# All tiles written out without a loop, the state product on the state itself in two array halves, and new orders on every engine

## Chip, cores and metric

One core of one Trainium2 chip runs the whole program. The metric is the device time of one execution in microseconds. TensorE (PE in the rows, with PEld for its weight loads), VectorE (DVE), ScalarE (ACT), GpSimd (POOL) and SyncE (SP), which issues all transfers, each work through a list of instructions of their own, in order. They wait for each other by semaphores.

## What is computed

An mLSTM layer with eight heads, in the role of cross attention, and then a gated feed-forward layer whose operands are rounded to blocks of FP4. Batch 8, sequence 1024, width 512, hidden width 1408.

```python
x = x + mlstm(layernorm(x), ctx, ctx, igate_w, igate_b, fgate_w, fgate_b, norm_w)
x = x + ffn(layernorm(x), w_gate, w_up, w_down)
# mlstm, per head of 64 columns: q from x, k = v = ctx
log_D = tril(log_f_cum[:, None] - log_f_cum[None, :] + ig[None, :])
C = (q @ k.T / 8) * exp(log_D - max_log_D)
h = C / (max(abs(C.sum(-1)), exp(-max_log_D)) + 1e-6) @ v     # then a norm per head
# ffn: quant() rounds blocks of 16 to the FP4 grid, times max/6 of the block
gate, y = quant(x) @ quant(w_gate).T, quant(x) @ quant(w_up).T
out = quant(silu(gate) * y) @ quant(w_down).T
```

## The kernel before

**Tiles.** The 8 x 1024 tokens are 64 tiles of 128 tokens. Tile t is the chunk t // 8 of the sequence of batch t % 8 (its slot). The attention is computed chunk by chunk: the pairs inside a chunk as a 128 x 128 matrix per head, and everything older by a state of 64 x 65 numbers per head (`St`, one per slot; the 65th column sums the weights). Heads come in four pairs (`HC` = 4); a pair's two heads lie on partitions 0 to 63 and 64 to 127.

**A tile's way.** Load x and ctx, layer norm, transposes (`pe_x_T`, `pe_c_T`), gates (`pe_gate_mm`, and for every four tiles together `pe_pick_mm`, scans on VectorE, `pe_row_T`), then the scores (`pe_qk`), the decay matrix `D` (ScalarE exponential, GpSimd mask, VectorE product with the scores), the output product `pe_u`, the state's update (`pe_st_mm`, `dve_Sd` decays the state, `dve_St` adds), the norm per head (uc, sq, vr, ve, sch, hn), the residual `x1`, the second layer norm, quantising to `xqs` (a high and a low f16 part, ending in `dve_x_lo`), a transpose by transfer to `xqT` (`sp_xqT`), the gate and up products (`pe_gu`, in three pieces of 512, 512 and 384 columns; its first matmul of each group of six is L482), silu and product (h), quantising again (h_t, h_q, h_qs, h_hi, h_lo), a transpose by transfer (`sp_hqT`, three pieces), the down product (`pe_down`, L597 to L599) and the store.

**Turns.** The work is pipelined by hand. In turn u each engine works on several tiles of different age: TensorE on the gate and up product of tile u-8, the transposes and gates of u-1, the output product and state of u-6, the down product of u-9, the scores of u-5. The order inside a turn is written out in `pe_turn`, `act_turn`, `pool_turn`, `dve_turn` and `sp_turn`. TensorE's is gu piece 0, c_T, x_T, row_T, gu 1, gates, gu 2, u, down 0, st_mm, down 1, qk, down 2. Ahead of turn 10 stand start lists written out by hand (`pe_start` and so on), in which the three weights are quantised and the first tiles begin. Turns 10 to 18 and 59 to 74 are straight code. Turns 19 to 58 are a loop of five rounds with eight turns each (`turns`); in it a `Tile` carries the loop's register j, and each semaphore value, and each address of a transfer, is register arithmetic (`Tile._plus`, `tokens`). In the loop and outside it the order is the same.

**The output product.** `pe_u` adds, into two PSUM banks (`U`), the product of the decayed queries `xw` with the state and that of `D` with the values. For the first it uses `Sbd`, a copy of the state in which a pair's two heads stand on the diagonal of a 128 x 130 block with zeros beside them, so that one matmul over all 128 rows serves two heads. `act_Sbd` makes that copy, in two instructions for each tile; `dve_Sd` may change the state once it is made. The scores (`pe_qk`, L500) have no such copy: they contract over 64 rows, even heads on the upper and odd heads on the lower half of the array, into two banks. `pe_st_mm` (L583) writes 64 columns of the array a head.

Of the kernel before, what the change touches and what calls it, by code (L numbers as in the profile page):

```python
# [27 lines left out]
class Tile:  # L28


    def __init__(self, first, j=None):
        self.first, self.j = first, j
# [4 lines left out]
    def live(self, total):  # L37
        return self.j is not None or 0 <= self.first < total

    def at_start(self, n):  # L40
        return self.j is None and self.first == n

    def has(self, back):
        return self.j is not None or self.first >= back

    def back(self, d):
        return Tile(self.first - d, self.j)

    def _plus(self, value, per_loop):
        return value if self.j is None else self.j * per_loop + value  # L50

    def done(self, back=0, k=1):

        return self._plus(k * (self.first - back + 1), 8 * k)

    def of(self, k, i):

        return self._plus(k * self.first + i + 1, 8 * k)

    def dma(self, ring, back=0):  # L60

        return self._plus(16 * ((self.first - back) // ring + 1), 16 * (8 // ring))

    def quads(self, back=0):

        return self._plus((self.first - back) // 4 + 1, 2)

    def quads_of(self, k, i, back=0):

        return self._plus(k * ((self.first - back) // 4) + i + 1, 2 * k)  # L70

    def quad(self):
        return self._plus(self.first // 4, 2)

    def chunk(self):
        return self._plus(self.first // 8, 1)


def mlstm_fp4_ffn(nc, x, ctx_in, ig_w, ig_b, fg_w, fg_b, norm_w, w_gate, w_up, w_down, out):
# [22 lines left out]
    def tokens(t):  # L102
        return bass.ds(t.chunk() * P + t.slot * S, P)

    with ExitStack() as stack:
# [48 lines left out]
        Sbd = sb("Sbd", [P, HC, 2, DA])  # L154
# [73 lines left out]
        def pair(t, n):  # L228
# [14 lines left out]
            "go", "fill", "const", "g_in", "g_sum", "gT_ps", "gT", "pick", "zero",  # L243
# [9 lines left out]
            "D", "xw", "vc", "vk", "qk", "u", "st_mm", "Sd", "St", "sq", "un",  # L253
# [13 lines left out]
        s_mask, s_C, s_uc, s_Sbd = ([sem(f"s_{k}{n}") for n in range(2)] for k in ("mask", "C", "uc", "Sbd"))  # L267
# [7 lines left out]
        LOOP0, LOOPS = 19, 5  # L275
        LAST = NT + 11
# [13 lines left out]

        def sp_wait(e, s, value):
# [1407 lines left out]
```

## Time and profile before

| | us |
|---|---|
| median of three runs | 1970.78 (1965.21 to 1971.99) |
| the profiled execution | 1977.65 |
| its span, first to last instruction | 1975.9 |
| mean granted TensorE clock | 0.971 of 2.4 GHz |

An engine's busy time counts its own instructions, without waits, branches and the issuing of transfers. A matmul's record begins when it begins to stream and goes on until its modelled end, so neighbours overlap; the distance between starts is what a matmul takes. An f32 product makes two weight loads and two matmul records, an f16 product one of each. An idle time is put down to what was last to arrive.

### The profile page before, as it was taken

What the parts mean: (1) busy time and instruction counts of PE and PEld (TensorE: products, weight loads), DVE (VectorE), ACT (ScalarE), POOL (GpSimd) and SP (SyncE); (2) the same over time, 40 slices, a digit from 0 to 9 for tenths busy, and PEclk for the clock granted to TensorE, in tenths of its full rate; (3) what the DMA queues carried; (4) which work ended last, traced back from release to release, by engine and by line L of the source; (5) the groups of instructions that cost most, each with busy time, mean ns of one, the idle gap of its engine ahead of it and who ended that gap; (6) DMA issues with size and microseconds to landing.
All of it is one profiled execution on the core that took longest, in us unless ns stands there. A gap on an engine that the chain in (4) does not pass through costs nothing. (4 is left out here: it accounts for less than half of the span.)

```text
span 1975.9 us, 41157 instructions
## 1 busy us (share of the span) xinstructions
PE 1829.6 (93%) x12001; PEld 1031.1 (52%) x12001; DVE 1455.9 (74%) x3213; ACT 1452.2 (73%) x2990; POOL 1167.6 (59%) x1189
## 2 busy tenths in 40 slices
PE   2448999999999999999999999999999999999997
PEld 1334555555555555554555555555555555555553
DVE  8788777777777677776777777777777777778784
ACT  5767687787877777786777777777777877776663
POOL 7675655656565656655565655656566555655652
PEclk9758999999999999999999999999999999999999
DMA  6844444444344434444354443444344444444423
GB/s 198 177 107 103 99 117 110 115 111 115 102 116 110 118 102 116 100 114 106 101 120 106 116 102 101 116 110 118 98 111 109 107 115 113 109 102 94 103 64 71
DMA packets 366406, 218.40 MB, mean 111 GB/s; under 512 B 299168, under 2 KB 305824, under 8 KB 366144
## 3 DMA queue, kind: packets, MB, share of 16 engines
q1 hardware_dynamic: 366144, 215.40, 43.9%
q8 instruction: 105, 1.72, 0.4%
q14 instruction: 157, 1.29, 0.2%
HBM read 126.45 MB, written 17.30 MB: 73 GB/s over the span
## 5 line engine op out<-in xcount | busy, mean ns | idle before, releaser
L1041 POOL TENSOR_TENSOR stage<-stage,hs 128x512 f32<-128x512 f32 (+1 forms) x192 | 224.3, 1168 | 437.5 <-DVE stage L1249 433.3
L482 PE MATMUL bank<-wgTh,xqT 128*128 128x512 f16 (+1 forms) x768 | 281.2, 366 | 27.1 <-DMA xqT<-xqs 23.3
L483 PE MATMUL bank<-wuTh,xqT 128*128 128x512 f16 (+1 forms) x768 | 280.0, 365 | 0.0
L484 PE MATMUL bank<-wgTl,xqT 128*128 128x512 f16 (+1 forms) x768 | 279.7, 364 | 0.0
L487 PE MATMUL bank<-wuTh,xqT 128*128 128x512 f16 (+1 forms) x768 | 279.7, 364 | 0.0
L485 PE MATMUL bank<-wuTl,xqT 128*128 128x512 f16 (+1 forms) x768 | 279.5, 364 | 0.0
L486 PE MATMUL bank<-wgTh,xqT 128*128 128x512 f16 (+1 forms) x768 | 279.3, 364 | 0.0
L597 PE MATMUL bank<-wdTh,work 128*128 128x512 f16 x704 | 268.8, 382 | 11.0 <-DMA work<-stage 11.0
L598 PE MATMUL bank<-wdTl,work 128*128 128x512 f16 x704 | 267.6, 380 | 0.0
L599 PE MATMUL bank<-wdTh,work 128*128 128x512 f16 x704 | 267.5, 380 | 0.0
L1303 DVE TENSOR_TENSOR stage<-stage 128x512 f16<-128x512 f32 (+1 forms) x192 | 156.9, 817 | 102.5 <-ACT stage L723 102.4
L855 ACT ACTIVATE work<-stage 128x512 bf16<-128x512 f32 (+1 forms) x192 | 114.0, 594 | 152.4 <-POOL stage L1094 139.8
L1268 DVE SCALAR_TENSOR_TENSOR stage<-bank,wfix,stage 128x512 f32<-128x512 f32 (+1 forms) x192 | 133.3, 694 | 121.9 <-ACT stage L733 120.8
L1260 DVE TENSOR_TENSOR D<-bank,D 128x512 f32<-128x512 f32 x128 | 88.2, 689 | 160.3 <-POOL D L1034 133.2
L1094 POOL TENSOR_TENSOR stage<-stage,hinv 128x512 f32<-128x512 f32 (+1 forms) x192 | 190.0, 991 | 10.7 <-DVE hinv L1334 10.7
L1029 POOL TENSOR_TENSOR sch<-ve,mhalf 128x8 f32<-128x8 f32 x64 | 106.2, 1659 | 105.6 <-DVE ve L1457 105.6
L733 ACT ACT_TABLE_LOAD x126 | 161.7, 1283 | 3.2 <-PE bank L487 1.1
L680 ACT ACTIVATE D<-mb,cols 128x128 f32<-128x128 f32 x512 | 156.3, 387 | 4.1 <-DMA mb<-max_dram 2.9
L1077 POOL TENSOR_TENSOR xn<-xn,xs 128x512 f32<-128x512 f32 x64 | 68.2, 1065 | 141.0 <-DVE xn L1315 141.0
L571 PE MATMUL bank<-vc,D 128*128 128x65 f32 x1024 | 147.1, 268 | 0.0
L733 ACT ACTIVATE stage<-bank,wfix 128x512 f32<-128x512 f32 (+1 forms) x192 | 124.7, 649 | 24.4 <-PE bank L487 22.6
L571 PEld LDWEIGHTS bank<-vc,D 128*128 128x128 f32 x1024 | 140.1, 198 | 0.0
(191 smaller groups left out, 4252.2 us busy)
## 6 DMA issues: line engine op xcount, KB each, us to landing
mb<-max_dram SPq DMA_DIRECT2D x64, 512.0 KB, 3.9
xb<-in_x_dram SPq DMA_DIRECT2D x64, 256.0 KB, 2.8
cf<-in_ctx_dram SPq DMA_DIRECT2D x64, 256.0 KB, 2.7
cn<-in_ctx_dram SPq DMA_DIRECT2D x64, 256.0 KB, 3.0
x<-in_x_dram SPq DMA_DIRECT2D x64, 256.0 KB, 3.1
wb<-warp_dram SPq DMA_DIRECT2D x128, 128.0 KB, 2.9
out_dram<-ob SPq DMA_DIRECT2D x64, 256.0 KB, 3.1
work<-stage SPq DMA_TRANSPOSE x192, 3.1
```

Of the source, the lines that this page charges most:

```text
L482: e.matmul(g[:, 0:w], hi, wgT[0][:, c, n0:n0 + w], start=first, stop=False)
L483: e.matmul(y[:, 0:w], hi, wuT[0][:, c, n0:n0 + w], start=first, stop=False)
L484: e.matmul(g[:, 0:w], hi, wgT[1][:, c, n0:n0 + w], start=False, stop=False)
L485: e.matmul(y[:, 0:w], hi, wuT[1][:, c, n0:n0 + w], start=False, stop=False)
L486: e.matmul(g[:, 0:w], lo, wgT[0][:, c, n0:n0 + w], start=False, stop=last)
L487: i = e.matmul(y[:, 0:w], lo, wuT[0][:, c, n0:n0 + w], start=False, stop=last)
L571: i = e.matmul(o[:, par, :], D[:, par, c, :], vc[t.parity][:, 2 * c + par, :], start=False, stop=(c % 2 == 1 and par == 1))
L597: e.matmul(DOWN[:, :], hi, wdT[0][:, c0 + c, :], start=(c0 + c == 0), stop=False)
L598: e.matmul(DOWN[:, :], hi, wdT[1][:, c0 + c, :], start=False, stop=False)
L599: i = e.matmul(DOWN[:, :], lo, wdT[0][:, c0 + c, :], start=False, stop=(c0 + c == IC - 1))
L733: e.activation(sl[:, n0:n0 + w], pair(t, n)[0][:, 0:w], ACT.Silu, scale=wfix[:, 0:1]).then_inc(s_silu[n], 1)
L1041: e.tensor_tensor(blocks(hx[:, n0:n0 + w]), blocks(hx[:, n0:n0 + w]), per_block(hs2[:, n0 // BLOCK:(n0 + w) // BLOCK]), ALU.mult).then_inc ...
```

## The change

It does four things.

1. `turns` is one straight list of turns, 10 to 75. `Tile` has no register, all semaphore values and addresses are constants, and the helper `sp_wait` with its extra semaphore increment is gone, as is GpSimd's in `pool_mask`.
2. `Sbd`, `act_Sbd` and the filling of `Sbd` are gone. `pe_u` multiplies `xw` with `St` directly, a head at a time, over 64 rows: four heads first, on alternating halves and into alternating banks, then D's eight products, then the other four heads. TensorE waits for its own first group ahead of the last. `dve_Sd` now waits for u.
3. The orders inside a turn are new on every engine. TensorE's differs by x_T, row_T, c_T in place of c_T, x_T, row_T. SyncE takes x_in, cn_in (one turn later than before), rows_out (one turn later), the store (one turn later), hqT 0, hqT 1, x1_in, mb_in, hqT 2, xqT, c_in, wb_in. VectorE has hn at the end of its turn and not early in the next; GpSimd and ScalarE are below.
4. The start lists are new. They hold the same work but for a few steps at the seam to the first turn.

```diff
         def tokens(t):
-            return bass.ds(t.chunk() * P + t.slot * S, P)
+            return slice(t.first // 8 * P + t.slot * S, t.first // 8 * P + t.slot * S + P)
...
         def turns(e, turn):
-            for u in range(FIRST, LOOP0):
-                turn(e, u, None)
-            with e.Fori(0, LOOPS) as j:
-                for i in range(8):
-                    turn(e, LOOP0 + i, j)
-            for u in range(LOOP0 + 8 * LOOPS, LAST):
-                turn(e, u, None)
+            for u in range(FIRST, LAST):
+                turn(e, u)
...
-            e.wait_ge(s_Sbd[0], t.done())
-            e.wait_ge(s_Sbd[1], t.done())
+            if t.at_start(0):
+                e.wait_ge(S_["zero"], 1)
+            if t.has(8):
+                e.wait_ge(S_["St"], t.done(8))
             e.wait_ge(S_["xw"], t.done())
             e.wait_ge(S_["vc"], t.done())
             e.wait_ge(s_C[0], t.done())
             e.wait_ge(s_C[1], t.done())
+
+
+            def inter(c, par, **flags):
+                r = slice(par * DH, (par + 1) * DH)
+                return e.matmul(U[c // 2][:, c % 2, par, :], xw[r, c, :], St[t.slot][r, c, :], **flags)
+
+            for c in range(2):
+                even, odd = inter(c, 0, start=(c == 0), stop=False), inter(c + 2, 1, start=(c == 0), stop=False)
+            even.then_inc(S_["u_first"], 1)
+            odd.then_inc(S_["u_first"], 1)
             for c in range(HC):
-                o = U[c // 2][:, c % 2]
-                e.matmul(o.rearrange("p r d -> p (r d)"), xw[:, c, :], Sbd[:, c, :, :].rearrange("p r d -> p (r d)"),
-                         start=(c % 2 == 0), stop=False)
                 for par in range(2):
-                    i = e.matmul(o[:, par, :], D[:, par, c, :], vc[t.parity][:, 2 * c + par, :], start=False, stop=(c % 2 == 1 and par == 1))
+                    e.matmul(U[c // 2][:, c % 2, par, :], D[:, par, c, :], vc[t.parity][:, 2 * c + par, :], start=False, stop=False)
+            e.wait_ge(S_["u_first"], t.of(2, 1))
+            for c in range(2):
+                inter(c + 2, 0, start=False, stop=(c == 1))
+                i = inter(c, 1, start=False, stop=(c == 1))
             i.then_inc(S_["u"], 1)
...
-        def act_Sbd(e, t, par):
-            if t.at_start(0):
-                e.wait_ge(S_["zero"], 1)
-            if t.has(8):
-                e.wait_ge(S_["St"], t.done(8))
-            if t.has(1):
-                e.wait_ge(S_["u"], t.done(1))
-            r = slice(par * DH, (par + 1) * DH)
-            e.copy(Sbd[r, :, par, :], St[t.slot][r, :, :]).then_inc(s_Sbd[par], 1)
...
         def dve_Sd(e, t):
             if t.at_start(0):
                 e.wait_ge(S_["zero"], 1)
-            e.wait_ge(s_Sbd[0], t.done())
-            e.wait_ge(s_Sbd[1], t.done())
+            e.wait_ge(S_["u"], t.done())
             e.wait_ge(S_["wb_in"], t.of(32, 31))
```

The orders of a turn after the change, a name with the tile's age behind it where that isn't plain:

- ScalarE: nm2, xh, sq2, warp, x1c, hz 2, var2, hz 0, xT, cols, cT, silu 0, ln1_sum, h_hi 0, gpart, silu 1, ln1_mean, xz, f_abs, f_neg, mean, f_exp, ig, h_hi 1, f_log, silu 2, uc 0, uc 1, ln1_sq, sq, ln1_var, h_hi 2, x_hi, D, hz 1. Before, ln1_sq and ln1_var stood ahead of uc, and warp ahead of D.
- GpSimd: hx 2, mask 1, hx 0, rs2, xw, h_qs 0, vc, vk, h_qs 1, x_qs, h_qs 2, un, ln1_rs, sch, hx 1, ln1_nb, mask 0. Before: mask 0, hx 0, h_qs 0, rs2, vc, h_qs 1, xw, vk, h_qs 2, x_qs, ln1_rs, un, ln1_nb, sch, hx 1, mask 1, hx 2.
- VectorE: hpw, x1, C 0, hr, h_t 1, C 1, hs2, h_t 2, h_t 0, xam, sd2, h_q 0, xt, xi, h 0, out, h_lo 0, xn, h_q 1, ham 0, h 1, x_t, xs, osc, x_q, h_lo 1, F, h_q 2, a, h 2, ham 1, ham 2, nr_neg, Sd, ht, nr, vr, h_lo 2, nq, St, n2, x_lo, M, mc, ve, hs, row3, hinv, hn, hm, row4. Before, from nr_neg on: nr_neg, vr, nr, ht, nq, h_lo 2, n2, x_lo, ve, hs, St, hm, hinv, C 1, h_t 1, row4, with Sd early in the turn.
- In SyncE's start list the gates' 13 transfers (`sp_g_in`) stand behind 17 blocks of weights; before, they stood behind 6. Block 9 of the last weight goes ahead of the first tile's rows_out, mb_in and wb_in; before, it stood behind wb_in. In VectorE's, the largest value of the first weight (w_wm, w_top, w_pw) is taken ahead of its first rounding, and before, behind it.

## Rows read from the trace of the kernel before

**Rows 1.** The page: busy time of each engine, then TensorE's busy tenths in 40 slices

```profile
PE 1829.6 (93%) x12001; PEld 1031.1 (52%) x12001; DVE 1455.9 (74%) x3213; ACT 1452.2 (73%) x2990; POOL 1167.6 (59%) x1189
...
PE   2448999999999999999999999999999999999997
```

**Rows 2.** Stretches: us, busy time of PE PEld DVE ACT POOL, PEclk, DMA share, GB/s

```profile
0.00:212.53 212.53, 109.05 (x669) 71.62 (x669) 170.41 (x296) 136.84 (x311) 139.65 (x166) 0.77 0.60 146
212.53:463.31 250.78, 249.74 (x1683) 141.48 (x1684) 183.68 (x426) 195.30 (x405) 152.29 (x154) 1.00 0.43 110
463.31:1611.46 1148.15, 1121.96 (x7491) 629.02 (x7489) 835.53 (x1900) 874.73 (x1811) 674.32 (x680) 1.00 0.44 109
1611.46:1779.50 168.04, 167.06 (x1128) 94.71 (x1128) 122.89 (x285) 130.16 (x268) 100.60 (x101) 1.00 0.43 108
```

**Rows 3.** Timeline of PE, first matmul of tiles 3, 4 and 5: start, us, line

```profile
240.02 0.38 PE L482 MATMUL bank<-wgTh,xqT 128*128 128x512 f16 x1
...
267.50 0.38 PE L482 MATMUL bank<-wgTh,xqT 128*128 128x512 f16 x1
...
296.47 0.38 PE L482 MATMUL bank<-wgTh,xqT 128*128 128x512 f16 x1
```

**Rows 4.** Waits of PE in the loop, 463 to 1611: us, times, longest

```profile
PE bank L482 <- DMA xqT<-xqs: 21.0, 30, 2.8
```

**Rows 5.** Timeline of DVE, first instruction behind a jump back of the loop

```profile
921.44 0.15 DVE L1344 TENSOR_SCALAR hpw<-hm 128x1 int32<-128x1 int32 x1 [2.90 <-issue]
```

**Rows 6.** Timeline of PE in one turn outside the loop, around u, st_mm and qk

```profile
1683.86 0.39 PE L568 MATMUL bank<-Sbd,xw 128*128 128x130 f32 x2
...
1686.48 0.38 PE L597 MATMUL bank<-wdTh,work 128*128 128x512 f16 x1
...
1688.85 0.38 PE L599 MATMUL bank<-wdTh,work 128*128 128x512 f16 x1
1689.16 0.69 PE L583 MATMUL bank<-vk,cn 128*64 128x65 f32 x16
1689.78 0.39 PE L597 MATMUL bank<-wdTh,work 128*128 128x512 f16 x1
...
1692.17 0.38 PE L599 MATMUL bank<-wdTh,work 128*128 128x512 f16 x1
1692.47 1.16 PE L500 MATMUL bank<-xT,cT 64*128 64x128 f32 x16
1693.57 0.39 PE L597 MATMUL bank<-wdTh,work 128*128 128x512 f16 x1
```

**Rows 7.** Timeline of PE's weight loads in the same u

```profile
1683.97 0.53 PEld L571 LDWEIGHTS bank<-vc,D 128*128 128x128 f32 x4
1684.41 0.30 PEld L568 LDWEIGHTS bank<-Sbd,xw 128*128 128x128 f32 x2
```

**Rows 8.** Timeline of DVE in the same turn: Sd

```profile
1671.77 0.42 DVE L1413 TENSOR_TENSOR St<-St,wb 128x260 f32<-128x260 f32 x1
```

**Rows 9.** Same turn: ACT, DVE, the queue; then median times to landing

```profile
1685.36 0.71 ACT L795 ACTIVATE junk<-xb,nm 128x512 bf16<-128x512 f32 x1
...
1686.68 0.65 ACT L875 COPY uc<-bank 128x260 f32<-128x260 f32 x2 [0.29 <-PE bank L571]
...
1689.49 0.68 DVE L1319 TENSOR_TENSOR xqs<-xn,xqs 128x512 f16<-128x512 f32 x1
...
1691.71 1.65 SPq L345 DMA_TRANSPOSE xqT<-xqs  x1
...
xqT<-xqs SPq DMA_TRANSPOSE x64, 3.5
...
mb<-max_dram SPq DMA_DIRECT2D x64, 512.0 KB, 3.9
```

**Rows 10.** Timeline of DVE in the start: two waits for blocks of weights

```profile
14.42 1.28 DVE L1468 TENSOR_REDUCE xqs<-stage 128x32 f32<-128x512 f32 x2 [3.38 <-DMA stage<-in_L_ffn_w_gate_dram]
...
93.48 0.69 DVE L1468 TENSOR_REDUCE xqT<-stage 128x32 f32<-128x512 f32 x1 [4.61 <-DMA stage<-in_L_ffn_w_down_dram]
```

More of the change, by code:

```diff
@@ L28, with __init__ @@
 class Tile:
-    def __init__(self, first, j=None):
-        self.first, self.j = first, j
+    def __init__(self, first):
+        self.first = first
     slot = property(lambda self: self.first % 8)
@@ L266, in mlstm_fp4_ffn @@
         s_gu, s_silu, s_h = ([S_[f"{k}{n}"] for n in range(NP)] for k in ("gu", "silu", "h"))
-        s_mask, s_C, s_uc, s_Sbd = ([sem(f"s_{k}{n}") for n in range(2)] for k in ("mask", "C", "uc", "Sbd"))
+        s_mask, s_C, s_uc = ([sem(f"s_{k}{n}") for n in range(2)] for k in ("mask", "C", "uc"))
         s_hx, s_hz, s_h_t, s_h_q, s_h_qs, s_h_hi = ([sem(f"s_{k}{n}") for n in range(NP)] for k in ("hx", "hz", "h_t", "h_q", "h_qs", "h_hi"))
@@ L304, in sp_x1_in @@
             if t.has(4):
-                sp_wait(e, S_["out"], t.done(4))
+                e.wait_ge(S_["out"], t.done(4))
             e.dma_start(x1[t.slot % 4][:, :], x_rows[tokens(t), :]).then_inc(s_x1_in[t.slot % 4], 16)
@@ L318, in sp_x_in @@
             if t.has(1):
-                sp_wait(e, S_["x_T"], t.done(1))
+                e.wait_ge(S_["x_T"], t.done(1))
             e.dma_start(xb[:, :], x_rows[tokens(t), :]).then_inc(S_["x_in"], 16)
@@ L323, in sp_c_in @@
             if t.has(1):
-                sp_wait(e, S_["c_T"], t.done(1))
+                e.wait_ge(S_["c_T"], t.done(1))
             e.dma_start(cf[:, :], c_rows[tokens(t), :]).then_inc(S_["c_in"], 16)
@@ L330, in sp_mb_in @@
             if t.has(1):
-                sp_wait(e, S_["D"], t.done(1))
-            sp_wait(e, S_["max_out"], t.dma(4))
+                e.wait_ge(S_["D"], t.done(1))
+            e.wait_ge(S_["max_out"], t.dma(4))
             e.dma_start(mb[:, :, :].rearrange("p h s -> p (h s)"),
-                        max_dram[bass.ds(t.done() - 1, 1), :].broadcast_to([P, NH * P])).then_inc(S_["mb_in"], 16)
+                        max_dram[t.first:t.first + 1, :].broadcast_to([P, NH * P])).then_inc(S_["mb_in"], 16)
         def sp_xqT(e, t):
@@ L341, in sp_xqT @@
                 e.wait_ge(S_["w_wi"], 6 * len(PARTS))
-            sp_wait(e, S_["x_lo"], t.done())
+            e.wait_ge(S_["x_lo"], t.done())
             if t.has(2):
-                sp_wait(e, s_gu[2], t.done(2))
+                e.wait_ge(s_gu[2], t.done(2))
             e.dma_start_transpose(xqT[t.parity][:, :, :], xqs[:, :, :].rearrange("p s d -> p (s d)")).then_inc(s_xqT[t.parity], 16)
@@ L348, in sp_rows_out @@
             if t.slot % 4 == 3:
-                sp_wait(e, S_["gate"], t.quads_of(3, 2))
-                four = bass.ds(t.done(3) - 1, 4)
+                e.wait_ge(S_["gate"], t.quads_of(3, 2))
+                four = slice(t.first - 3, t.first + 1)
                 e.dma_start(max_dram[four, :].rearrange("n (h s) -> (n h) s", h=NH), mw[:, 0, :]).then_inc(S_["max_out"], 16)
-                sp_wait(e, S_["warp"], t.quads())
+                e.wait_ge(S_["warp"], t.quads())
                 e.dma_start(warp_dram[four, :].rearrange("n (h s) -> (n h) s", h=NH), mw[:, 1, :]).then_inc(S_["warp_out"], 16)
@@ L368, in sp_cn_in @@
             if t.has(1):
[L369 to L370 removed]
+                e.wait_ge(S_["vc"], t.done(1))
+                e.wait_ge(S_["st_mm"], t.done(1))
             e.dma_start(cn[:, :], c_rows[tokens(t), :]).then_inc(S_["cn_in"], 16)
@@ L492, in pe_qk @@
             e.wait_ge(S_["cT"], t.done())
+            if t.at_start(0):
+                e.wait_ge(S_["xT"], T[4].done())
+                e.wait_ge(S_["cT"], T[4].done())
             if t.has(1):
@@ L1139, in pool_zero @@
                 e.memset(St[i][:, :, :], 0.0)
-            e.memset(Sbd[:, :, :, :], 0.0)
             for i in range(2):
```

547 lines of the change are left out of this document (263 added, 284 removed).

## The prediction, made before the changed kernel ran

> **What bounds the kernel now.** I read the busy shares and the slices first: TensorE is busy for 93% of the span and, after its first tenth, stands at 9 in nearly every slice, while VectorE has 74%, ScalarE 73% and GpSimd 59% [rows 1]. So TensorE is the bound, apart from the start. The busy times by stage say more [rows 2]: in two stretches, 212.53 to 463.31 us and 1611.46 to 1779.50, TensorE is idle for 1.0 us each, and between them, in 1148.15 us, for 26.2 us. All three stretches begin and end on the first matmul of a tile's gate and up product (L482), and their clock is 1.00, which is the level of 2.4 GHz. The middle stretch is the loop: turns 19 to 58, whose L482 belongs to tiles 11 to 50.
>
> The starts of L482 give the length of a turn outside the loop [rows 3]: 267.50 - 240.02 = 27.48 us, and 296.47 - 267.50 = 28.97 us in every fourth turn, which also has the gates' pick and a transpose. Forty loop turns, ten of them of the long kind, should take 30 x 27.48 + 10 x 28.97 = 1114.1 us. They took 1611.46 - 463.31 = 1148.15 [rows 2]. The same sum for the first stretch gives 7 x 27.48 + 2 x 28.97 = 250.3 against 250.78 measured, and for the third 4 x 27.48 + 2 x 28.97 = 167.9 against 168.04. So the same turn, in the same order, costs **34.1 us more inside the loop**, and nothing outside it. The list of waits names what is late there: the transposed activations xqT, 21.0 us in 30 waits [rows 4]. The jump back shows as VectorE standing for 2.9 us with nothing to wait for [rows 5], and the rest comes from the register arithmetic ahead of each wait and each transfer.
>
> **The change part by part.**
>
> *The loop goes: -34.1 us.* All waits and addresses become constants, as they are today in the turns outside the loop. Those turns are straight code already, 9 before it and 16 behind it, and reach the floor of 27.48, so more of such code should bring no cost of its own. The Trainium skill (Runtime: NRT & Kernel Launch, section Instruction fetch mechanics) says that a taken branch out of the current window forces a fetch before execution goes on; the 2.9 us agree with that.
>
> *The state product: +0.52 us a turn.* Today one pe_u has 4 products with Sbd and 8 with D, each of two f32 passes, so 24 weight loads with their matmuls. It runs from 1683.86 to 1686.48, which is 2.62 us, or 0.109 a pass, although the passes over Sbd stream 130 columns and those over D only 65 [rows 6]. Four loads for D take from 1683.97 to 1684.41, 0.11 each [rows 7]. So the f32 weight load of 128 columns sets the pace, not the streaming. Taking Sbd's 8 loads away is worth 8 x 0.109 = 0.87 us. In their place come 8 products on 64 rows each, so 16 passes, in two groups of 8 with D's 16 passes between them. The nearest row is the score product L500, also 64 rows by 128 columns in two row halves: 16 passes from 1692.47 to 1693.57. Before it, the last L599 began at 1692.17 and streams 0.216 (eleven steps from L597 at 1686.48 to L599 at 1688.85), so it ended at 1692.38. From there to the next full matmul it is 1.19 us. If the halves pair up, that is 8 steps of 0.112 (the same weight load) and 0.29 us of loss at the two ends. L583, tiled by columns, shows the same loss: 1688.85 + 0.216 = 1689.07 to 1689.78 is 0.71 us for 8 steps, which at 0.0585 us (half the columns to load) leaves 0.24. pe_u today has no such loss: L568 follows L487 without a gap, its weights loaded in advance. A group of four pairs then costs 4 x 0.112 + 0.24 to 0.29, less some 0.03 as only 65 columns stream: about 0.70. New pe_u: 2 x 0.70 + 16 x 0.109 = 3.14, against 2.62, so +0.52.
>
> Bounds: if the pairs step as fast as L583's (0.0585), a group costs 0.47 and pe_u grows by 0.07. If the halves don't pair, it is 8 x 0.109 + 0.29 = 1.16 a group and +1.4. I take +0.52, since L500 has the same rows and columns. Of 64 tiles, the first four have their pe_u in the start list, so 60 are on the path: 60 x 0.52 = **+31.2 us**.
>
> The Trainium skill (TensorEngine Tiling (Array Packing), section Key Properties) says that a change of tiling mode, not just of tile, drains the engine. That rule speaks against this change, which enters and leaves the halves twice a tile, and the trace agrees (the gap of 0.09 us ahead of L500 and L583). The same page's Theoretical Speedup promises up to 2x for two row tiles.
>
> *The new wait inside pe_u* (u_first) is for TensorE's own first four products, which D's 1.75 us put well behind: 0. D's products, the stores and the removed memset of Sbd cost nothing new. *Sbd's two copies* leave ScalarE, 0.4 us each, off the path: 0.
>
> *Sd waits for u now* instead of the copies, and stands behind nr_neg, which waits for the copy of u anyway. Sd is 0.42 us [rows 8]; behind it on VectorE are ht, nr, vr, h_lo, St. St must be done before L500. I place it at 4.0 us after the end of u; L500 begins 6.0 after it (1692.47 - 1686.48). So 0, with 2 us to spare.
>
> *The orders* decide whether TensorE keeps its floor. What is late in the loop is xqT, so I follow that chain from the end of u, called U (1686.48) [rows 9]. Before: the copy of u starts at U+0.2, x_lo (L1319) at U+3.0, the transfer xqT is issued at U+5.2 and lands about 3.5 us later (its median), U+8.7. The next turn begins at U+9.07. So there are 0.35 us to spare, and a loop that delays the chain by more costs TensorE directly. After: ln1_sq (L795, 0.71 plus its read) comes between uc and sq, and Sd and St come before x_lo. That puts vr at U+2.35, h_lo at U+3.0, St at U+3.65 and the end of x_lo at U+4.75, instead of U+3.6. But on the queue cn_in no longer stands between the last hqT and xqT: hqT is issued at U+3.65, is 1.25 us long, and xqT follows at U+5.05. Landing at U+8.55, with 0.5 us to spare. xqT for TensorE's next turn is late only if my chain is short by more than that. cn_in now follows x_in, at about 6 us into the turn and lands at 9; vc, vk and h_qs behind it on GpSimd wait for it, but the products that need them come after 16. mb_in stands behind the second hqT (17 us into the turn), lands 3.9 us later, and D wants it at 23. rows_out is a turn later and reads rows long ready; wb_in is last and is needed in the next turn. Each of them: 0.
>
> *The start: -4 us.* Up to 212.53 us VectorE is busy for 170.4 us [rows 2]; adding up the new start list with the old durations gives the same within 1 us. So only its 42 us of idle time can move. Two waits of it are for weights whose transfers stand behind others: 3.38 us, behind the gates' 13 transfers, and 4.61 us, behind wb_in [rows 10]. In the new list both are issued ahead of those. Against it, the first tile's scale (w_top, w_pw) is now asked for at once and waits for TensorE, some 1.5 us, and pe_u takes longer there too. Taken: -4; bounds -14 (all waits of VectorE for transfers gone) and +8 (one of TensorE's long waits more). *The end*: the last turns and the final chain keep their order: 0, with 2 us either way.
>
> **Sum** against the profiled execution (1977.65 us with 1975.9 of span): -34.1 + 31.2 - 4 = -6.9, so 1970.8. That execution is 6.9 us above the median of the runs, 1970.78. The median after is therefore 1970.78 - 6.9 = **1963.9**, own range 1952 to 1976. A measurement of this kernel can tell 0.3%, 5.9 us, from no change.
>
> **The rivals.**
> *Cheap halves.* The pairs overlap fully and the passes cost what L583's do: 60 x 0.07 = 4 instead of 31, so 1970.78 - 34.1 + 4.2 - 4 = 1937. For it: 65 columns and not 128. Against it: the D passes stream 65 columns as well and still take 0.109.
> *xqT late (slower).* The chain behind u, 1.15 us longer on VectorE, ends after the last down product. The point from which it decides is xqT landing later than U+9.07, 0.5 us beyond my estimate. At 1 us beyond it each turn loses 0.5 us, 55 turns x 0.5 = 27, hence 1991. For it: today's margin is as thin, and a small delay in the loop cost 34 us. Against it: the queue is clearer and the turn itself is longer.
> *Halves in series (slower).* 60 x 1.4 = 84: 2017. Against it: L500's 16 passes in 1.1 us.
> *The loop's loss stays.* Straight code stalls too: 1964 + 34 = 1998. The two stretches outside the loop speak against it.
> *The start moves by more than 8 us* either way.
>
> **How the numbers follow.** The forecast has 0.55, of which faster 0.30, same 0.21, slower 0.04. Cheap halves 0.13, all faster. xqT late 0.16 (slower 0.14, same 0.02). Halves in series 0.04 and the loop's loss 0.02, slower. The start by more than 8 us 0.10 (faster 0.04, same 0.03, slower 0.03). Together: faster 0.47, same 0.26, slower 0.27. The likeliest time is 1964. The range reaches down to the cheap halves and up to xqT late by a whole microsecond: 1935 to 1991.
>
> **What would show it.** In the middle the starts of L482 (its line in the new kernel) 28.0 us apart and 29.5 in every fourth turn, alike from tile 2 to 56, with no wait for xqT: both terms right. 27.55 apart: cheap halves. Above 28.3 with waits for xqT: that rival. The new pe_u from its first pass to the first down matmul 3.1 us, with gaps of 0.09 us around each group. The first L482 of tile 2 at about 208.5 us instead of 212.53. I am wrong if the new orders open a wait that today's profile doesn't contain, or if the loss at the change of tiling is not the same for f32 passes next to each other.

## The result, and the profile after

The kernel became slower. The changed kernel takes 1994.42 us (median, 1992.03 to 1998.71) against 1970.08 us of the kernel before (1965.21 to 1971.99). The ratio is 1.013, with a 95% interval of 1.0104 to 1.0155. The forecast was 1964 us, with a range up to 1991.

First the page of the changed kernel: its span, the busy times and TensorE's tenths. They answer to [rows 1].

```profile
span 1993.4 us, 38894 instructions
...
PE 1854.5 (93%) x12513; PEld 1042.9 (52%) x12513; DVE 1591.2 (80%) x3213; ACT 1375.8 (69%) x2864; POOL 1234.5 (62%) x1188
...
PE   1438999999999999999999999999999999999997
```

TensorE is still the bound, busy for 25 us longer. VectorE has the same 3213 instructions as before and is busy for 135 us longer with them; the last section comes back to this. Now the stretches, cut at the first gate product (L461 here, L482 before) of tiles 2 and 57, with the columns of [rows 2]: first the changed kernel, then the kernel before, cut at the same two tiles (its first stretch is in [rows 2]).

```profile
0.00:216.34 216.34, 109.31 (x700) 72.50 (x701) 173.44 (x301) 136.41 (x307) 142.03 (x165) 0.96 0.56 142
216.34:1794.77 1578.43, 1560.81 (x10740) 875.34 (x10741) 1263.63 (x2609) 1127.61 (x2368) 987.83 (x932) 1.00 0.42 108
1794.77:1993.40 198.63, 184.37 (x1074) 95.03 (x1072) 154.13 (x305) 111.78 (x190) 104.60 (x93) 0.98 0.34 82
```

```profile
212.53:1779.50 1566.97, 1538.77 (x10300) 865.21 (x10301) 1142.10 (x2611) 1200.19 (x2482) 927.21 (x933) 1.00 0.44 109
1779.50:1975.90 196.40, 181.78 (x1034) 94.30 (x1033) 143.34 (x306) 115.22 (x198) 100.77 (x92) 0.98 0.35 82
```

So of the 17.5 us between the two profiled executions, 3.8 came in the start, 11.5 in the middle and 2.2 at the end. The middle is 55 turns, and it splits further. The undisturbed turn is the one without a late transfer. In the kernel before it is 27.48 us, 27.59 behind a long one, and 28.98 for a long one; 28, 13 and 14 of these make 1533.8 us. In the changed kernel these are 28.08, 28.18 and 29.57, or 1566.4. So

| middle, us | before | after |
|---|---|---|
| 55 undisturbed turns | 1533.8 | 1566.4 |
| above that | 33.2 | 12.0 |
| together | 1567.0 | 1578.4 |

The halves added 32.6, the 33.2 above the undisturbed turns went, and 12.0 came that no step of the sum had. The waits of TensorE in this middle name them (us in total, times, longest):

```profile
PE bank L592 <- DMA work<-stage: 10.8, 15, 1.3
PE bank L532 <- ACT gpart L765: 6.8, 14, 0.5
PE bank L461 <- DMA xqT<-xqs: 2.1, 1, 2.1
```

The gates' 6.8 are in the kernel before as well. xqT, which [rows 4] had 30 times, is late once, at the very edge. In its place the down product waits (L592): its third piece of transposed data, the third hqT, is late in 15 of the 55 turns, by 0.7 us on average.

### The profile page after: what moved, and what is told of

It is laid out like the page before. It is cut to its first block and busy times, and to the rows that moved or that the text cites. A ratio compares the mean times of both kernels' runs of the same rounds, so it can differ in the third digit from the quotient of the medians.

```text
span 1993.4 us, 38894 instructions
## 1 busy us (share of the span) xinstructions
PE 1854.5 (93%) x12513; PEld 1042.9 (52%) x12513; DVE 1591.2 (80%) x3213; ACT 1375.8 (69%) x2864; POOL 1234.5 (62%) x1188
## 5 line engine op out<-in xcount | busy, mean ns | idle before, releaser
L1025 POOL TENSOR_TENSOR stage<-stage,hs 128x512 f32<-128x512 f32 (+1 forms) x192 | 189.3, 986 | 206.9 <-DVE stage L1233 206.3
L592 PE MATMUL bank<-wdTh,work 128*128 128x512 f16 x704 | 269.5, 383 | 22.2 <-DMA work<-stage 22.1
L461 PE MATMUL bank<-wgTh,xqT 128*128 128x512 f16 (+1 forms) x768 | 278.9, 363 | 4.7 <-DMA xqT<-xqs 4.7
L466 PE MATMUL bank<-wuTh,xqT 128*128 128x512 f16 (+1 forms) x768 | 278.0, 362 | 0.0
L1078 POOL TENSOR_TENSOR stage<-stage,hinv 128x512 f32<-128x512 f32 (+1 forms) x192 | 210.5, 1098 | 5.8 <-DVE hinv L1318 5.8
L1061 POOL TENSOR_TENSOR xn<-xn,xs 128x512 f32<-128x512 f32 x64 | 106.3, 1661 | 103.9 <-DVE xn L1299 103.9
L1228 DVE SCALAR_TENSOR_TENSOR stage<-work,stage 128x512 f32<-128x512 bf16 (+1 forms) x192 | 138.8, 723 | 19.1 <-ACT work L841 17.8
L729 ACT ACTIVATE stage<-bank,wfix 128x512 f32<-128x512 f32 (+1 forms) x192 | 124.8, 650 | 33.2 <-PE bank L466 31.7
L1215 DVE TENSOR_TENSOR un<-un,sch 128x512 f32<-128x512 f32 x64 | 98.7, 1542 | 57.2 <-POOL sch L1014 57.2
L1233 DVE SCALAR_TENSOR_TENSOR stage<-work,stage 128x512 f32<-128x512 bf16 (+1 forms) x192 | 142.7, 743 | 0.1
```

The lines of the kernel that those rows point to most:

```text
L461: e.matmul(g[:, 0:w], hi, wgT[0][:, c, n0:n0 + w], start=first, stop=False)
L466: i = e.matmul(y[:, 0:w], lo, wuT[0][:, c, n0:n0 + w], start=False, stop=last)
L592: e.matmul(DOWN[:, :], hi, wdT[0][:, c0 + c, :], start=(c0 + c == 0), stop=False)
L729: e.activation(sl[:, n0:n0 + w], pair(t, n)[0][:, 0:w], ACT.Silu, scale=wfix[:, 0:1]).then_inc(s_silu[n], 1)
L1025: e.tensor_tensor(blocks(hx[:, n0:n0 + w]), blocks(hx[:, n0:n0 + w]), per_block(hs2[:, n0 // BLOCK:(n0 + w) // BLOCK]), ALU.mult).then_inc ...
L1078: e.tensor_tensor(blocks(hx[:, n0:n0 + w]), blocks(hb[:, n0:n0 + w]), per_block(hinv[:, n0 // BLOCK:(n0 + w) // BLOCK]), ALU.mult).then_in ...
```

## The experiments

All times are medians. Kernels whose numbers are compared ran on one chip, or are compared through the kernel before, which ran beside each: 1975.09 us beside e1 to e4, 1969.96 beside e5 to e7, 1970.65 beside e8 to e10, 1971.14 beside e11 and e12. "The middle" is the same 55 turns throughout, and its excess is what it takes above its undisturbed turns.

### The parts, one by one: e1 and e2

e1 is the kernel before with its loop written out, and nothing else.

```
-            for u in range(FIRST, LOOP0):
-                turn(e, u, None)
-            with e.Fori(0, LOOPS) as j:
-                for i in range(8):
-                    turn(e, LOOP0 + i, j)
-            for u in range(LOOP0 + 8 * LOOPS, LAST):
+            for u in range(FIRST, LAST):
                 turn(e, u, None)
```

> The kernel before with its loop written out and nothing else: same orders, same block diagonal copy. Theory (the loop cost what its turns lack to the floor): every turn of the middle takes 27.48 us, 28.97 in every fourth, no waits for xqT, and the time falls by 34 us to about 1936. Rival (long straight code has a cost of its own, such as instructions that arrive late): turns above the floor in the middle and a time of 1950 or more.

e2 is the changed kernel with the block diagonal product back, its two copies on ScalarE behind act_hz(t9, 0).

```
-            for c in range(2):
-                even, odd = inter(c, 0, ...), inter(c + 2, 1, ...)
...
+                e.matmul(o.rearrange("p r d -> p (r d)"), xw[:, c, :], Sbd[:, c, :, :].rearrange("p r d -> p (r d)"),
+                         start=(c % 2 == 0), stop=False)
```

> The kernel after with the old product (block diagonal copy Sbd, made on ScalarE behind hz 0, and one matmul over 128 rows for two heads); straight code and new orders stay. Theory (the array halves cost 0.6 us a turn): turns of 27.5 and 29.0 us instead of 28.08 and 29.57, pe_u 2.6 us instead of 3.2, and 1994 - 60 x 0.6 = 1958. The waits for the third hqT (13 us in all) stay, since both its issue and the down product hang on the end of u. Rival (the new orders or straight code are what costs, the halves are neutral): 1985 or more.

Measured: e1 1958.42 us, ratio 0.9922 (0.9895 to 0.9949), so 17 us faster and not 34: the rival's side. e2 1960.38 us, ratio 0.9924 (0.9900 to 0.9948), as its theory had it. The spans make a ladder from the kernel before to the changed one: the loop away 1975.9 to 1956.1 (-19.8), the new orders and start lists to 1960.1 (+4.0), the halves to 1993.4 (+33.3). So the halves are the largest loss, near their price, and the loop gave 14 us less than its step of the sum. Of the 4.0, 3.3 are in the start, where tile 2 begins at 216.85 us and not at 213.56. In the middle e1 and e2 are alike: both have an excess of 14.0 us (1547.88 and 1547.80), at different places; first e1, then e2:

```profile
PE bank L477 <- DMA xqT<-xqs: 11.1, 12, 2.1
PE bank L545 <- ACT gpart L774: 6.8, 14, 0.5
```

```profile
PE bank L580 <- DMA work<-stage: 11.8, 12, 2.0
PE bank L533 <- ACT gpart L763: 6.8, 14, 0.5
PE bank L462 <- DMA xqT<-xqs: 1.5, 2, 1.1
```

Straight code is thus not free of the loop's waits. In e1 xqT is late by 1 us and more in the turns of tiles 13, 15, 17 and 19, in none before, by less in the odd ones up to 31, by 1 us again at 44 and 48, and by 0.7 at 52 and 56: a pattern that drifts.

### What makes a transfer late in one turn and not in the next: e6

The trace has one kind of traffic that comes in such a rhythm, the packets of instructions. The DMA view of two stretches of the changed kernel: first tile 17's turn, whose third hqT was issued at 669.99 and made TensorE wait for 1.07 us, then tile 18's, with hqT issued at 699.21 and no wait. The columns are as on the page; of the issues, the last number is the time to landing.

```profile
q8 instruction: 1, 0.02, 1.3%
...
work<-stage SPq DMA_TRANSPOSE x1, 4.5
xqT<-xqs SPq DMA_TRANSPOSE x1, 4.2
```

```profile
q1 hardware_dynamic: 1908, 0.58, 57.0%
q14 instruction: 1, 0.01, 0.4%
...
work<-stage SPq DMA_TRANSPOSE x1, 3.1
xqT<-xqs SPq DMA_TRANSPOSE x1, 3.1
```

Queue 8 brings 16 KB each time, and between two of its packets TensorE executes 256 recorded instructions on average in the written-out kernels: it is TensorE's own code. Queue 14 brings instructions too, in packets of 8 KB and less; whose they are was not asked. The 3.1 us of tile 18 are not the undisturbed time either. In the 32 turns of the changed kernel whose third hqT met no packet of either queue it landed in 2.73 to 2.77 us. A stretch of e2, in tile 19's turn:

```profile
work<-stage SPq DMA_TRANSPOSE x1, 2.7
```

In e2, tile by tile, a packet of queue 8 starts 1.8 to 2.6 us after the issue of the third hqT in the turns of tiles 21, 23, 25, 27, 29, 31, 52, 54 and 56. There the transfer lands after 4.2 to 5.2 us, and the down product begins right behind it; in all other turns the product begins at most 3.8 us after the issue, and in most at 3.35, its undisturbed place. (What I expected of e6 counts eight such turns; tile 56's, late by 0.8 us, is the ninth.) Four turns have 1552 TensorE instructions, 6 packets and 16 instructions over, so the packets creep through the turn by 16 instructions in four turns. That made a forecast possible: put 48 instructions in front of everything, and the late turns must move. TensorE stands idle in the start for 16 us, so this costs nothing.

```
             if t.at_start(0):
                 e.wait_ge(S_["const"], 2)
+                for _ in range(96):
+                    e.wait_ge(S_["const"], 2)
```

(two such waits are packed into one instruction)

> e2 with 48 waits that are already met, each one instruction, ahead of TensorE's first product in the start, where it stands idle for 16 us. Nothing else differs, so every turn holds the same work. In e2 a 16 KB instruction packet comes once in 256 TensorE instructions, and a quad of turns has 1552 of them, so the packets drift slowly through the turn. Theory (late down products are those whose transfer meets such a packet about 2 us after its issue): the packets come 48 instructions earlier in each turn, so the late turns are no longer those of tiles 21 to 31 (odd), 52 and 54, but those of tiles 9 to 19 (odd) and 40 to 50 (even), 10 to 12 instead of 8; the time is 1 to 6 us above e2. Rival (the delays come from something tied to the tiles or to other transfers): the late turns stay 21 to 31, 52 and 54, and the time is that of e2.

Measured: 1964.52 us, ratio 0.9971 (0.9956 to 0.9986), against e2's 0.9924 (0.9900 to 0.9948). In the traces the middle is 1551.80 us against 1547.80, so 4.0 us longer, of which 2.7 are twelve late turns for nine; the ratios say 9, of which the traces don't show the rest. The turns with a late third hqT by over 0.8 us are those of tiles 9, 11, 13, 15, 17, 19, 40, 42, 44, 46, 48 and 50: the twelve of the forecast, and no other. The forecast did not have two turns, of tiles 5 and 38, in which the transfer behind it, xqT, was late by 0.8 and 1.2 us; e2 has one such, of tile 17, by 1.1. TensorE's waits in two stretches show it in the profile. In 745 to 1065 us (tiles 21 to 31), e2 and then e6:

```profile
PE bank L580 <- DMA work<-stage: 7.4, 6, 2.0
```

```profile
PE bank L582 <- DMA work<-stage: 0.4, 1, 0.4
```

and in 410 to 725 us (tiles 9 to 19), e2 and then e6:

```profile
PE bank L580 <- DMA work<-stage: 0.7, 2, 0.4
```

```profile
PE bank L582 <- DMA work<-stage: 7.4, 7, 2.1
```

Nothing but the place of the code in its pages had moved. So the packet is the cause, and when it starts decides. In the middles of the seven traces with the new orders (the changed kernel, e2 to e6 and e12), 39 packets of queue 8 started 1.7 to 2.2 us after the issue of a third hqT, and 38 of these transfers landed after 4.2 to 5.2 us. Of 38 whose packet started 2.2 to 3.0 us after the issue, 16 did; the others landed within 2.95. In e6's tile 5, for one, the packet came 2.34 us after the issue, the third hqT landed in 2.75, and it was xqT, issued 1.3 us behind it, that took 4.4. In the changed kernel ten of the 15 waits for the third hqT have such a packet, 9.7 of the 10.8 us; the other five, 1.1 us, have one of queue 14, which made the transfer land after 3.6 to 3.8 us. How a packet holds up a transfer, by a DMA engine that both use or otherwise, isn't shown.

### Margin: e7, e9, e5

If a landing is 1 to 2 us late, it matters only where the transfer has less to spare. e7 is e1 with one swap on SyncE's queue; e9 is the same swap with the loop kept.

```
-            if t5.live(NT):
-                sp_cn_in(e, t5)
             if t7.live(NT):
                 sp_xqT(e, t7)
+            if t5.live(NT):
+                sp_cn_in(e, t5)
```

> e1 (the kernel before, its loop written out) with one swap on the queue: the transfer of xqT is issued ahead of cn_in instead of behind it, so some 0.65 us earlier. Theory (e1's middle stood 15.6 us above TensorE's floor only because xqT landed late in the turns where an instruction packet met it): the waits for xqT in the middle fall from 12 us to 2 to 6, time 1946 to 1952 us. Rival (the transfer's own slowness under the packet, or VectorE's x_lo, sets when xqT lands, not the queue ahead): less than 3 us gained, 1956 or more.

> The kernel before with its loop kept and the one swap of e7: xqT is issued ahead of cn_in. Theory (most of the loop's 34 us were waits for an xqT with 0.35 us to spare, and the jumps themselves cost little more than they delay it): the gain is 12 to 20 us, 1950 to 1958 us, and what is left against e7 is the jumps, 8 to 16 us. Rival (the loop's cost is the jumps and the register arithmetic, which only written-out code takes away): less than 6 us gained, 1964 or more.

Measured: e7 1942.03 us, ratio 0.9862 (0.9846 to 0.9878), the fastest kernel here, 28 us under the kernel before and faster than its theory had it. e9 1953.17 us, ratio 0.9911 (0.9890 to 0.9933), in its theory's range. e7's swap issues xqT 0.64 us earlier; its middle is 1534.91 us, 1.1 above the undisturbed turns, and its waits there beside the gates', followed by e9's, are

```profile
PE bank L592 <- DMA work<-stage: 0.8, 1, 0.8
PE bank L477 <- DMA xqT<-xqs: 0.3, 1, 0.3
```

```profile
PE bank L482 <- issue: 6.9, 4, 2.2
...
PE bank L482 <- DMA xqT<-xqs: 0.3, 1, 0.3
```

So of the loop's 33.2 us the jumps themselves, four of them seen here at L482, are 7 to 8 (e9's middle, 1542.30, less e7's), and the other 25 were xqT with too little to spare. The trace of the kernel before shows which turns these are. In those of the jumps (tiles 18, 26, 34 and 42) xqT was late by 2.2 to 2.8 us, 10.2 us in all. In 15 odd ones between tiles 13 and 49 a packet of queue 8 started 0.2 to 0.8 us after the issue of xqT, which then landed after 3.9 to 4.8 us and not 3.4. With the loop kept, one line moved gave as much as writing all 64 tiles out (e9 and e1), and both together gave e7.

e5 is e2 with more to spare for the third hqT: dve_Sd behind the third h_lo, where dve_St stands already, ln1_sq and ln1_var behind x_hi.

> The written-out kernel with the old block diagonal product (as e2) and the two moves of e3: Sd and St behind the last h_lo on VectorE, ln1_sq and ln1_var behind x_hi on ScalarE. Theory (a turn is TensorE's floor of 27.48 us plus what transposed data come late by, and the moves issue the third transfer of each turn some 0.35 to 0.45 us earlier): turns 27.48 and 28.97, waits for the transposed work tiles in the middle from about 15 us down to 6 or less, 8 to 10 us less than e2: about 1951 us. Rival (the delays sit in the transfers and grow with them, margin bought is margin lost): within 2 us of e2, 1959 to 1962.

Measured: 1950.08 us, ratio 0.9900 (0.9883 to 0.9917), where e2 had 0.9924; the excess in the middle falls from 14.0 to 6.0 us, as expected. The changed kernel's orders can be mended as well, but they don't catch up with e7.

### The halves by themselves: e4, e10, e11

e4 is the changed kernel with all eight 64-row products ahead of D, with a wait for its own first four between the two groups, so that TensorE enters and leaves the halves once and not twice.

```
+            e.wait_ge(S_["u_first"], t.of(2, 1))
+            for c in range(2):
+                inter(c + 2, 0, start=False, stop=False)
+                inter(c, 1, start=False, stop=False)
             for c in range(HC):
                 for par in range(2):
-                    e.matmul(U[c // 2][:, c % 2, par, :], D[:, par, c, :], ...)
-            e.wait_ge(S_["u_first"], t.of(2, 1))
...
```

> The kernel after with all eight 64-row products ahead of D's: first four, a wait for them, the other four, then D. The mode of the array changes twice a tile in pe_u instead of four times. Theory (each stay in the halves loses 0.25 to 0.29 us at its ends, as at L500): one such loss goes, and the wait of TensorE for its own first four costs some 0.2 us, as nothing lies between: pe_u 3.1 to 3.2 us against 3.21, and 1988 to 1996. Rival (the loss hangs on D's own weight loads or on the number of products, not on the change of mode): pe_u 3.4 us and above, 2006 and more.

Measured: 2002.82 us, ratio 1.0142 (1.0118 to 1.0166), between the two expectations. The timelines of one pe_u, changed kernel and then e4:

```profile
692.18 0.33 PE L466 MATMUL bank<-wuTh,xqT 128*128 128x384 f16 x1
692.44 0.66 PE L554 MATMUL bank<-St,xw 64*128 64x65 f32 x8
693.03 2.00 PE L562 MATMUL bank<-vc,D 128*128 128x65 f32 x16
694.96 0.66 PE L554 MATMUL bank<-St,xw 64*128 64x65 f32 x8
695.55 0.39 PE L592 MATMUL bank<-wdTh,work 128*128 128x512 f16 x1
```

```profile
694.10 0.33 PE L466 MATMUL bank<-wuTh,xqT 128*128 128x384 f16 x1
694.35 1.42 PE L554 MATMUL bank<-St,xw 64*128 64x65 f32 x16
695.70 2.00 PE L566 MATMUL bank<-vc,D 128*128 128x65 f32 x16
697.54 0.38 PE L593 MATMUL bank<-wdTh,work 128*128 128x512 f16 x1
```

From L466 to the first down product it is 3.37 us in the changed kernel and 3.44 in e4, so the wait cost as much as the change of tiling it saved and 0.05 us a turn more, 2.8 us in the 55; another 2 are late transfers. One group without the wait was not tried.

e10 puts the halves into e7, whose orders have margin. Sd has to wait for u now and stands behind x_lo.

```
-            e.wait_ge(s_Sbd[0], t.done())
-            e.wait_ge(s_Sbd[1], t.done())
+            e.wait_ge(S_["u"], t.done())
...
                 dve_x_lo(e, t7)
+            if t6.live(NT):
+                dve_Sd(e, t6)
```

> e7 (written out, xqT ahead of cn_in, the orders of before otherwise) with the state product in halves, without Sbd and its copies; Sd stands behind x_lo on VectorE. Theory (the halves cost TensorE 0.60 us a turn and nothing else; the 13 us of new waits of the changed kernel came from its orders): turns 28.08 and 29.57 without waits for transposed data in the middle, 60 x 0.60 = 36 us above e7, 1976 to 1980. Rival (the halves bring waits of their own, as they also lengthen the chain behind u): 1985 or more, with waits of the down or the gate product in the middle.

Measured: 2119.08 us, ratio 1.076 (1.0734 to 1.0786): the rival's side, with waits of the down product (94.3 us in the 55 turns), and far above both. The queue's timeline in one turn shows that they don't come from the halves' own chain:

```profile
711.41 1.23 SPq L309 DMA_TRANSPOSE work<-stage  x1
718.38 1.11 SPq L357 DMA_DIRECT2D wb<-warp_dram  x2
719.67 1.23 SPq L309 DMA_TRANSPOSE work<-stage  x1
```

The load of wb waits for Sd of the tile before, as Sd is its buffer's last reader. It stood between the second and the third hqT, and with Sd late it held the third hqT until 719.67. In the changed kernel wb_in is the last of the queue's turn, and this is why it has to be. e11 moves it there:

```
             if t9.live(NT):
                 sp_hqT(e, t9, 1)
-            if t5.live(NT):
-                sp_wb_in(e, t5)
...
                 sp_rows_out(e, t1)
+            if t5.live(NT):
+                sp_wb_in(e, t5)
```

> e10 with wb_in issued last in each turn of the queue instead of between the second and the third hqT. In e10 wb_in waited there for Sd of the tile before, which in this kernel comes only after u, and held back the third hqT: TensorE waited for it in every turn, 111.6 us in all. Theory (the halves themselves cost TensorE 0.60 us a turn and nothing else): turns 28.08 and 29.57, few waits in the middle, 30 to 38 us above e7, 1973 to 1980. Rival (the halves bring waits for transposed data of their own): 1985 or more.

Measured: 2000.74 us, ratio 1.0142 (1.0115 to 1.0169), by its time the rival's side. But by its trace the middle is clean, 28.08 and 29.57 us a turn:

```profile
PE bank L544 <- ACT gpart L776: 6.8, 14, 0.5
PE bank L476 <- DMA xqT<-xqs: 2.4, 1, 2.4
```

It is 1568.81 us, 33.9 above e7's, of which the halves are 55 x 0.595 = 32.7. Another 20 us are in the start (tile 2 begins at 233.50 us and not at 213.09), where I had moved Sd next to St in the list without working it out, which was not tested by itself, and 5 are behind the middle. So the halves bring no waits of their own in a turn; their price is 0.6 us of TensorE.

### Where the third hqT lost its margin: e3, e12

e3 is the changed kernel with e5's two moves. e12 has only the first of them, Sd.

```
                 dve_nr_neg(e, t6)
-                dve_Sd(e, t6)
...
                 dve_h_lo(e, t9, 2)
             if t6.live(NT):
+                dve_Sd(e, t6)
                 dve_nq(e, t6)
```

> The kernel after with two steps moved in every turn: on VectorE Sd stands behind h_lo 2 and no longer ahead of vr, and on ScalarE ln1_sq and ln1_var stand behind x_hi and no longer around sq. Theory (the third hqT is issued 3.45 us ahead of its down product, and any transfer that takes longer holds TensorE): it is issued about 1.1 us earlier, TensorE's waits for it fall from 22 to under 9 us (the last tiles' remain), and the time by 10 to 13 us to about 1982. Rival (the transfer's late landings don't depend on the margin, or they come back as waits for xqT or St): 1990 or more.

> The changed kernel with only Sd moved, from behind nr_neg to behind the third h_lo; ln1_sq and ln1_var stay ahead of sq on ScalarE (e3 moved both). In the changed kernel's trace the VectorE instruction that runs beside GpSimd's un (1.19 us) takes 1.38 us (Sd), in e3's it is ht (1.20 instead of 0.19): whichever it is ends when un ends. Theory (the place beside un costs the chain the length of un, whatever stands there, so moving Sd saves its own 0.42 less a little, and sq, which ends before un does, is not what vr waits for): all of e3's gain, third hqT at 22.3 us into the turn as in e3, 1983 to 1989 us. Rival (sq behind ln1_sq holds vr up): half of it or less, third hqT at 22.5 or later, 1990 or more.

Measured: e3 1986.59 us, ratio 1.0061 (1.0036 to 1.0085); e12 1985.70 us, ratio 1.0072 (1.0046 to 1.0097). The changed kernel has 1.0130; by the spans e3 gains 10 us and e12 11, so no part of the move on ScalarE can be seen. In both the third hqT is issued 22.34 us into the turn instead of 22.68 (e3's theory had 1.1 us earlier), and the excess in the middle falls from 12.0 to 3.0 and 3.8 us. Those 0.34 us do more than add to the time to spare: most packets of queue 8 now start when the transfer is about to land, and where ten made it late in the changed kernel, three do in e3 and five in e12. This is the VectorE and GpSimd timeline behind u in the changed kernel, and then in e12:

```profile
696.54 1.38 DVE L1396 TENSOR_TENSOR St<-St,wb 128x260 f32<-128x260 f32 x1
697.85 0.19 DVE L1307 TENSOR_SCALAR ht<-ham 128x88 f32<-128x88 f32 x1
...
698.64 0.54 DVE L1287 TENSOR_TENSOR stage<-stage 128x384 f16<-128x384 f32 x1
...
696.45 1.19 POOL L1088 TENSOR_TENSOR un<-uc,nw 128x512 f32<-128x512 f32 x1 [0.80 <-ACT uc L861]
```

```profile
717.95 1.21 DVE L1307 TENSOR_SCALAR ht<-ham 128x88 f32<-128x88 f32 x1
...
719.75 0.54 DVE L1287 TENSOR_TENSOR stage<-stage 128x384 f16<-128x384 f32 x1
720.22 0.41 DVE L1396 TENSOR_TENSOR St<-St,wb 128x260 f32<-128x260 f32 x1
...
717.91 1.18 POOL L1088 TENSOR_TENSOR un<-uc,nw 128x512 f32<-128x512 f32 x1 [0.97 <-ACT uc L861]
```

Sd takes 1.38 us beside un and 0.41 elsewhere; in e12 it is ht that takes 1.21 and not 0.19. In 54 of the 55 turns it is so. Whichever stands there ends 0.1 to 0.3 us after un does.

### The base of the sum: e8

e8 is the kernel before once more, unchanged.

> The kernel before once more, unchanged, for its profile. In the sum of the prediction its profiled execution stood 6.9 us above the median of the unprofiled ones, while every written-out kernel's profiled time so far lies within 2 us of its median. Theory (profiling costs the looped kernel some time at its jumps): the profiled execution is again 5 to 9 us above the median of the unprofiled ones. Rival (that one execution was slow by chance): within 3 us.

Measured: 1971.89 us over 8 runs, its profiled execution 1974.37, 2.5 above that. So nothing shows that profiling slows the loop, and the first profiled execution, 1977.65 us, looks like a slow one by chance. Tile 2 began at 210.17 us here and at 212.53 there: the start alone moves by 2 us from one execution to the next.

## Why the prediction was wrong

Two steps failed together: "the loop goes: -34.1", by its claim that straight code brings no cost of its own, and "the orders" at 0, by its claim that no transfer is late. In their place stand 12.0 us of waits for the third hqT. The start, forecast at -4, went the other way.

**The loop, -34.1 us.** Alone it gave 19.8 us between the spans and 17 between the medians (e1), as 14.0 us of late xqT stay in the middle. In the changed kernel all 33.2 us at xqT are gone, but the new orders did that, and late landings of another transfer stand in their place; that this term looks right in size there is luck. The step said that more straight code "should bring no cost of its own", since the turns outside the loop reach the floor. Those were 15 turns. In 12 of them no packet of TensorE's code came near xqT; in the other three (tiles 51, 53 and 55) one started 0.2 to 0.3 us after its issue, and it landed after 3.7 to 3.8 us, just ahead of its use at 3.82. In e1 packets meet it in other turns. The step also put the loss down to the jump and to register arithmetic. e9 shows 7 to 8 us of jumps, and 25 of xqT with 0.35 us to spare. The Trainium skill (Runtime: NRT & Kernel Launch, section Instruction fetch mechanics) gives the block as 16 KiB or 256 instructions, which the packets here agree with, and calls the cost of crossing one "mostly hidden". For TensorE itself it is: in e2 the turn of tile 13, with a packet 3.9 us behind the issue of the third hqT, is 27.59 us long, its undisturbed length. For a transposing transfer with under 1 us to spare it isn't.

**The halves, +31.2 us.** Right: 0.60 us a turn against 0.52. The two groups take 0.69 us each (0.70 forecast). The rest is in D's sixteen passes, which now stand behind a change of tiling: from 693.029 to 694.865 us they take 1.84 us, not 1.75, as the first step is 0.161 us long and the others 0.112. In the middle and at the end that came to 34.8 us (32.6 and 2.2), not 31.2.

**Sbd's copies, Sd, St.** In sum at nothing, which holds as far as St and qk go. Sd itself was mis-sized, 0.42 us [rows 8] for 1.38.

**The orders, 0.** Beside straight code alone the new orders cost nothing in the middle (an excess of 14.0 us in e1 and in e2), but that is one late transfer for another. What failed is the claim that TensorE keeps its floor. The chain behind u was forecast well: h_lo at U+3.0 (measured 3.09), the third hqT issued at U+3.65 (3.66), the end of x_lo at U+4.75 (4.72), xqT issued at U+5.05 (4.97). I then asked whether xqT lands in time, since it was what [rows 4] showed late, and it does. I did not ask the same of the third hqT on the line above it. Its down product begins 3.45 us behind the issue, where the kernel before left it 3.90, and it lands after 2.75 when undisturbed. So it has 0.7 us to spare and had 1.15, and the packets that come near it start 1.8 to 2.8 us behind its issue, where in e1 they start 2.3 to 2.9 behind and none makes TensorE wait. A margin of 0.35 us for xqT had cost 25 us in the loop; the change took that weak point away and made a lesser one next to it, for 12.0 us. The rival "xqT late" was near, but it named another transfer and a delay that is the same in each turn.

**The start, -4 us.** Wrong in sign. Five executions with the old list (the kernel before, e8, e1, e7, e9) reach tile 2 at 210.17 to 213.56 us, seven with the new one (the changed kernel, e2 to e6, e12) at 213.00 to 216.85, some 3 us later in the mean. The granted clock up to there does not order these times: it was 0.77 in e8's (210.17 us) and 0.98 in e1's (213.56). The two waits of VectorE for weights did shrink, from 3.38 to 1.20 us and from 4.61 to 1.33, but others came. VectorE is also busy for 3.0 us longer up to tile 2. Which of these sets the end of the start was not taken apart, and the cause stays open.

**The base.** The sum started from an execution that stood 7.6 us above the median of the runs, and e8's did by 2.5. The profiled executions differ by 17.5 us, the medians by 24.3. Of the 31 us between forecast and result, 7 are this, 12 the third hqT (by the steps on the loop and the orders together), 8 the start, 3 to 4 the halves, and 1 is what the loop's excess measured less than its term.

## What to carry to other kernels

When an order is changed, work out the time to spare for every transfer that the bounding engine waits for, not only for the one that is late today, and ask for 1 to 2 us where the transfer transposes: in e7, with 1.15 us for the third hqT and 1.4 for xqT, 1.1 us of the 14.0 were left. Turns that run clean in a short stretch prove little: the fetching of code drifts through the turn and meets a thin margin only in some. And before a loop is written out, look for the queue entry that stands needlessly in front of the late transfer.

## What the runs showed of the hardware

TensorE's code arrives in 16 KB packets, in the written-out kernels one for each 256 of its instructions (101 in the changed kernel), and 105 in the kernel before. A packet that started 1.7 to 2.2 us after the issue of a third hqT made it land after 4.2 to 5.2 us in 38 of 39 cases with the new orders; with none it takes 2.75. Later ones did so in 16 of 38 cases there, and in none of 53 in the three executions with the loop (the kernel before, e8, e9), where the next transfer, xqT, was late instead. Why they differ is open. Moving all code by 48 instructions moved which turns were slow, from nine of them to the twelve that had been worked out.

VectorE and GpSimd hold each other up. Sd, with two inputs in SBUF, and ht, with one, last 1.38 and 1.21 us where they begin beside GpSimd's un, and 0.41 and 0.19 elsewhere. The other way, GpSimd's xn takes 1.91 us in the 40 turns of the changed kernel in which it begins while VectorE is at an instruction with two inputs, and 1.06 in the 14 in which VectorE begins one after it. The reduction ham is not held up, 0.67 us beside GpSimd's xn in the kernel before:

```profile
1685.24 0.67 DVE L1273 TENSOR_REDUCE ham<-stage 128x32 f32<-128x512 f32 x1
...
1685.40 1.06 POOL L1077 TENSOR_TENSOR xn<-xn,xs 128x512 f32<-128x512 f32 x1 [1.82 <-DVE xn L1315]
```

The Trainium skill (SBUF — State Buffer, section SBUF: two separate sides) calls the port pair of the two an "exclusive lock", held for the whole instruction, and names as VectorE's side of it instructions with two SBUF inputs or in a mode that uses both ports. Sd and ham agree; that ht runs in such a mode no run here shows. The new orders pair such instructions more often, and VectorE's 3213 instructions take 1591 us and not 1456; in e11, with the halves and the old orders, they take 1439. Most of the difference is in three of them: Sd, the product of un and sch (1.54 us a turn for 0.79) and h, whose 512-column pieces take 1.04 us and not 0.68 in 123 of 219 cases, those that begin beside an instruction of GpSimd.
